# Added matrix products in the first steps of the softmax and forget attention stages

## The reference

```python
x = x + softmax_attention(layernorm(x))     # 16 heads of 16, rotary positions, softmax over 512 keys
x = x + mixture(layernorm(x))               # 64 experts, top 8, capacity 128, and a shared expert
x = x + forget_attention(layernorm(x))      # linear attention with a decay, over the 16 sequences as steps
x = x + mixture(layernorm(x))               # the same weights again
```

## Time and profile before

| | us |
|---|---|
| median of 3 executions | 2755.16 |
| lowest and highest | 2754.28, 2756.10 |
| the profiled execution | 2756.48 |
| its span, first to last instruction | 2754.8 |
| TensorE busy | 2424.5 (88%) |
| VectorE busy | 1737.0 (63%) |
| ScalarE busy | 1272.0 (46%) |
| GpSimd busy | 1128.4 (41%) |

### The profile page before, as it was taken

The page is one execution under the profiler, slowest core; times in us unless marked ns, Lnnn a source line. Parts: engine busy times, 40 slices in busy tenths (PEclk is TensorE's granted clock), DMA queues, the critical chain, the costliest instruction groups (busy, mean ns, idle before and its releaser), DMA issues. The chain is left out here.

```text
span 2754.8 us, 47087 instructions
## 1 busy us (share of the span) xinstructions
PE 2424.5 (88%) x14506; PEld 1327.5 (48%) x14506; DVE 1737.0 (63%) x3661; ACT 1272.0 (46%) x2564; POOL 1128.4 (41%) x1350
## 2 busy tenths in 40 slices
PE   8996899999999999699878883899999979888885
PEld 5653233323333333366456662566666556556663
DVE  7996887788778877288422222688888669632221
ACT  3452576676666667444223220545545424322221
POOL 6888000100000010133136663677777723226664
PEclk9997799999999999899989995999999989999997
DMA  5554323232232321255439982011111036537985
GB/s 165 189 190 160 103 91 95 83 92 84 89 92 88 97 81 47 72 164 195 146 102 247 233 194 54 16 36 36 36 38 30 21 120 202 177 101 193 236 224 104
DMA packets 289374, 325.30 MB, mean 118 GB/s; under 512 B 28944, under 2 KB 270752, under 8 KB 289184
## 3 DMA queue, kind: packets, MB, share of 16 engines
q1 hardware_dynamic: 257536, 274.49, 32.4%
q0 software_dynamic: 27136, 46.16, 8.3%
q10 hardware_dynamic: 4512, 2.40, 0.3%
HBM read 217.23 MB, written 105.19 MB: 117 GB/s over the span
## 5 line engine op out<-in xcount | busy, mean ns | idle before, releaser
L672 DVE TENSOR_REDUCE a_row_max<-a_ps_m 128x2 f32<-128x1024 f32 x512 | 615.0, 1220 | 126.5 <-PE a_ps_m L570 124.4
L720 ACT ACTIVATE a_probs<-a_ps_s 128x512 f32<-128x512 f32 x1024 | 545.7, 600 | 293.7 <-PE a_ps_s L596 293.4
L596 PE MATMUL a_ps_s<-a_qs,a_ks 98*128 98x512 bf16 (+1 forms) x1024 | 319.1, 390 | 9.8 <-ACT a_probs L720 7.5
L611 PE MATMUL a_ps_o<-a_probs,a_va 128*32 128x512 f32 x2048 | 272.3, 604 | 0.8 <-ACT a_o_sb L729 0.8
L1511 POOL TENSOR_TENSOR b_spread<-b_decay,held_own_sb 128x512 f32<-128x512 f32 x256 | 269.1, 1084 | 8.6 <-DVE b_weight L1609 8.6
L570 PE MATMUL a_ps_m<-a_ks,a_qs 48*128 48x512 bf16 x1024 | 207.1, 401 | 45.6 <-DVE a_row_max L672 40.0
L570 PEld LDWEIGHTS a_ps_m<-a_ks,a_qs 48*128 48x128 bf16 x1024 | 49.3, 93 | 342.0 <-DVE a_row_max L672 169.4
L545 POOL DMA_DIRECT2D x<-a_xo x32 | 23.5, 735 | 442.6 <-DVE a_xo L705 442.6
L1609 DVE TENSOR_TENSOR b_weight<-b_ps_s,b_spread 128x512 f32<-128x512 f32 x256 | 163.6, 681 | 17.9 <-PE b_ps_s L1744 17.9
L596 PEld LDWEIGHTS a_ps_s<-a_qs,a_ks 98*128 98x128 bf16 (+1 forms) x1024 | 69.8, 97 | 157.5 <-ACT a_probs L720 86.2
L516 POOL CAST a_high<-a_row_max 128x32 bf16<-128x32 f32 x32 | 6.7, 209 | 321.2 <-DVE a_row_max L672 321.2
(11 more groups left out here) (326 smaller groups left out, 5097.5 us busy)
## 6 DMA issues: line engine op xcount, KB each, us to landing
parts<-a_parts SPq DMA_DIRECT2D x16, 1536.0 KB, 6.2
a_qs<-parts SPq DMA_DIRECT2D x384, 64.0 KB, 2.2
a_ks<-parts SPq DMA_DIRECT2D x384, 64.0 KB, 2.2
m_w_gu<-in_L_ffn_w_gate_dram SPq DMA_DIRECT2D x64, 384.0 KB, 4.0
m_w_gu<-in_L_ffn_w_up_dram SPq DMA_DIRECT2D x64, 384.0 KB, 5.4
m_w_d<-in_L_ffn_w_down_dram SPq DMA_DIRECT2D x64, 384.0 KB, 6.7
rows<-m1f_row SPq DMA_DIRECT2D x16, 640.0 KB, 3.1
rows<-m2f_row SPq DMA_DIRECT2D x16, 640.0 KB, 3.1
```

The source lines that it names most:

```text
L596: nc.tensor.matmul(s_bank(name, step)[:], ks[u][0:K_ALL[e], h, t * P:(t + 1) * P], qs[u][0:K_ALL[e], h, :], start=True, stop=True).then_in ...
L611: last = nc.tensor.matmul(ps_o[VW * j:VW * (j + 1), :], va[n.u][:, t, (h0 + j) * VW:(h0 + j + 1) * VW], probs[:, group % 2, j, t, :], star ...
L672: nc.vector.tensor_reduce(row_max[:, n.k // 4 % 2, t, :, n.p % 4], m_bank(name, step)[:], AX.X, ALU.max).then_inc(m_drained, 1)
L720: nc.scalar.activation(probs[:, group % 2, j, t, :], s_bank(name, step)[:], ACT.Exp, scale=DK ** -0.5).then_inc(s_drained, 1)
```

## The change

Two places in TensorE's program get more products. No result of them is read, and they signal nothing; their banks are written again by the real products before anything reads them.

In `attention_mix`, behind the two products of each `max_products` call of steps 0 to 5 (four calls a step), three more of 48 partitions, 128 rows and 512 columns, bf16, one into each `ps_s` bank; they read the rows of `qs` and `ks` that the first of the two real products reads. That is 72 products.

In `forget_attention`, a new part `stay_busy` with lag 0 stands twice in TensorE's list, behind `project_values` and behind `turn_x`; in steps 0 to 10 it issues two bf16 products of 128 partitions, 128 rows and 512 columns into `ps_o`, of the bias operands `first_rows` and `b_terms`. That is 44 products. `first_rows` holds ones in three partitions and zeros in the others.

```diff
@@ attention_mix, max_products
                     last.then_inc(m_filled, 1)
+                    if isinstance(step.base, int) and step.base == 0 and step.k < L_S:
+
+                        rows = slice(ROW[0][0], ROW[0][0] + MAX_SLOTS * DK)
+                        for i in range(3):
+                            nc.tensor.matmul(ps_s[i][:], qs[u][rows, 2 * n.p, t * P:(t + 1) * P], ks[u][rows, 2 * n.p, :], start=True, stop=True)
                 return stage
@@ forget_attention, TensorE
+            def stay_busy(n):
+
+                if n < L_PV - 1:
+                    for _ in range(2):
+                        nc.tensor.matmul(ps_o[:].rearrange("p i a -> p (i a)"), first_rows[:], b_terms[:, 0:4 * P], start=True, stop=True)
+
...
-            in_turn([(L_VF, project_values), (L_S, scores), (L_PV, mix_values), (L_TURN, turn_x), (L_OUT, turn_output), (L_FEED, project_features),
+            in_turn([(L_VF, project_values), (0, stay_busy), (L_S, scores), (L_PV, mix_values), (L_TURN, turn_x), (0, stay_busy), (L_OUT, turn_output),
+                     (L_FEED, project_features),
                      (L_OUT, turn_att), (L_UPTO, sum_logs), (L_OUT, project_out)])
```

## The result

| | before | after |
|---|---|---|
| median of 22 executions each, us | 2754.4 | 2761.1 |
| lowest and highest | 2743.2, 2758.3 | 2750.0, 2770.5 |
| ratio, with its 95% interval | | 1.0024 (1.0013 to 1.0035) |
| the profiled execution, us | 2756.5 | 2762.0 |

A forecast was written before the change was run, and what follows sets the result against it. TensorE, busy 88% of the span, was taken as the bound, with VectorE pacing the softmax fill. Softmax +12.1 and forget -2.4 gave +9.7 us: 2764.9 by the median, stated range 2749 to 2770.

The forecast's parts named there:

- The clock in the softmax fill: Start of the softmax stage: granted clock stays at 0.50 despite the added products, through the first score and beyond.
- The price: Softmax fill: 1.70 us a slot for 24 slots, first score at 301.8 instead of 289.71, a loss of 12.1 us.
- The upper bound: Softmax fill: if weight loads show between products, 5.8 us more, a loss of 17.9.
- The lower end: Softmax stage: if the clock rises right away after the fill, 2.9 us less, a loss of 9.2.
- The forget part: Start of the forget stage: fillers raise the clock earlier, a gain of 2.4 us.
- Delay by ten products: Forget stage: ten fillers ahead of the first turn_x take 4.2 us and delay it by 2.2.
- Cycle: Forget fill: with the clock risen, turn_x starts every 2.65 us, 1.3 less than before.
- Push in the last steps: Forget stage, steps 9 and 10: fillers push project_features by about 0.3 us each, 0.6 lost.
- A rise in both fills: Softmax and forget fills: rival, clock rises in both, 2.9 us won in softmax, 5.3 together, total 2749.9; chance 0.25.
- No rise in the forget stage: Forget stage: rival, fillers do not raise the clock there either, losses +12.1 and +3.5, total 2770.8; chance 0.10.
- A rise midway: Softmax fill: rival, clock rises after ten slots or so, -1.6 us, total 2753.6, no change; chance 0.08.
- the second rival: Forget stage: fillers do not act as work there either, +12.1 + 3.5 us, total 2770.8; chance 0.10.

The follow-up runs named there:

- e1: The change without stay_busy, softmax fillers alone, against the kernel before: ratio 1.0049 (1.0032 to 1.0065), +13.5 us.
- e4: The change with one fp32 product of 384 columns on 48 partitions replacing a slot's three fillers; against the kernel before: ratio 1.0020 (1.0001 to 1.0038).
- e10: The change with one filler instead of three in a softmax slot; against the kernel before: ratio 0.9991 (0.9973 to 1.0009).
- e11: The change with two fillers instead of three in a softmax slot; single execution, softmax stage 3.3 us longer than in the kernel before; no ratio given.
- e3: The change with softmax fillers on 128 partitions, of a bf16 copy of weights; against the kernel before: ratio 0.9982 (0.9964 to 0.9999).
- e2: The change without the softmax fillers, forget part alone, against the kernel before: ratio 0.9986 (0.9970 to 1.0001), -3.8 us.
- e8: The change with softmax fillers on 128 partitions, operands all zeros; one execution, softmax stage 873.6 us against 877.4 in the kernel before; no ratio given.
- e12: The change with 128-partition softmax fillers, ten more ahead, operand copied by ScalarE, forget fillers only in steps 0 to 8; against the kernel before: 1.0001 (0.9983 to 1.0018).
- e13: Ten 128-partition fillers before the first softmax pair, none in the slots; single execution, softmax stage 879.1 us against 877.4 in the kernel before; no ratio given.
- e6: The kernel before, unchanged, timed again against itself: ratio 1.0003 (0.9985 to 1.0020).
- e5: The whole change, timed again against the kernel before: ratio 1.0031 (1.0015 to 1.0048), +8.5 us.

## Why the prediction was right

**The clock in the softmax fill.** Forecast to stay at 0.50; it did, in all six profiles with 48-partition fillers (the change twice, e1, e4, e10 and e11). The reading that carried it was rows 2, where a nearly gapless 16.9 us had not raised it. The rule of the Trainium skill ("TensorE: Matmul & The Clock Gate", Part 1) that sustained activity releases the throttle, by which the result would have been 2749.9, didn't hold for this stream: 48 partitions kept busy for 42.6 us did nothing. The reading left two differences open, the partitions and fp32 against bf16; e3 and e4 settled it for the partitions. The rows also show when the clock does rise: in all eleven profiles in which it was low behind the first score, it rose between 0.3 us before and 2.3 us behind the first product with the values, which runs on 128 partitions (before: 306.5 and 306.57; after: 321.1 and 319.49). That these products raise it is likely by e3, but no run moves them alone.

**The price.** 1.70 us a slot forecast, 1.71 measured. First score 12.1 later forecast, 12.3 measured. The upper bound (weight loads that show, 17.9) wasn't reached for fillers on the partitions of the pair; with 128-partition fillers at 0.50 a slot was 1.93. The lower end (clock rises right behind the fill) wasn't either: it stayed low 18.5 us behind the first score, 1.6 more than before.

**The forget part.** Delay by ten products, 4.2: 4.24. Cycle 2.65: 2.69. Push in the last steps 0.3 each: `project_features` 0.42 further behind `turn_x`, and 0.56 for both steps in the sum (2.2 won at the first `project_features`, 1.6 at the first scores). The step that was mis-sized is the moment of the rise: I had it at the end of the ten products, it came 1.5 us behind, so the first cycle took 3.2 instead of 2.65 and the first `project_features` won 2.2 instead of 3.0. Gain against that profile: 1.6 instead of 2.4.

**What I missed.** The trace that I read had no dip of the clock behind the rise; two of three profiles of code without forget fillers have one, and rise 1.3 to 1.8 us later besides; together that is worth 2.3 to 2.6 us. On average the forget part therefore wins 3.4 rather than 1.6; the timing of e2 says 3.8, but its interval (-0.3 to 8.2) holds both. That and 12.9 in the softmax stage give 9.5 for the whole, nearly the 9.7 forecast. This closeness is in part luck: the loss was put 0.8 too low and the gain 1.0 too low, and the two cancel. The timings gave 6.7 (3.6 to 9.6) and 8.5 (4.1 to 13.2): 9.5 is at the edge of one and well inside the other. What keeps the first at 6.7 isn't settled: the experts stages scatter by 4 to 7 us from one execution of a kernel to the next.

**The rivals.** A rise in both fills: e3 shows what it is worth (3.7 us in the softmax stage, forecast 2.9), and that it needs another filler. The stretch behind the fill took 12.2 us there and not the 14.0 of the forecast: VectorE had gone on without a stop, so the 1.7 until its first reduction fell away. No rise in the forget stage: fell. A rise midway: none seen. The stated range ended at 2770, a little below the sum's own upper bound (2770.7) and the second rival (2770.8); the result didn't put that to the test.

## What to carry to other kernels

A filler keeps or raises TensorE's clock by what it runs on, so judge it by the rows in which the clock did and didn't rise, not by whether TensorE is busy: with 48 partitions at work it did nothing here, with 128, even of zeros, it did. Look separately at what raises the clock and at what holds it: pairs and scores held it once it was up (e3) and hadn't raised it in 16.9 us (rows 2). Price it as if it fails, at the low clock and in program order: a filler is free only while pair and fillers together stay under the pace of the engine that sets it (0.85 of 1.13 us here with one filler, 1.70 with three). And look for the next idle wait behind the padded stretch: 3.7 us without work gave everything back.

## What the runs showed of the hardware

- Granted clock 0.50 through 42.6 us of gapless products on 48 partitions, bf16 or fp32; 1.00 within 6.4 us with the same stream on 128 partitions, operands of zeros included (e3, e8).
- Pairs on 48 and scores on 98 and 112 partitions left the clock at 0.50 for 16.9 us (before, 289.6 to 306.5) and held it at 1.00 for 12.2 us in e3.
- The clock fell at 291.8 in a wait of TensorE that had begun at 288.6 (e12), at 262.8 with pairs alone behind a rise at 259.3 (e13), and 10 us behind a rise in a fill with waits, there for about 3 us only (e6).
- A VectorE cast of 128x512 fp32 to bf16 took 3.75 us beside a GpSimd memset; ScalarE's copy of the same 0.63.
- The same experts stage of the same kernel lasted 260.4 and 267.5 us in two executions. The clock falls at other places from one execution to the next, as at the end of the softmax stage, where that cost 4 us, or in its middle (e5); whether that is the cause of the scatter in the experts stages wasn't tried and stays open.
